# Cross-attention operands laid out and loaded per group of four sequences, three stage buffers, the loop written out

## The chip, the cores and the metric

The kernel runs on one core of one Trainium2 chip. The time is the device time in microseconds (us) of one execution; a profiled execution gives the span from the first to the last instruction. TensorE (PE) multiplies into PSUM, VectorE (DVE), ScalarE (ACT) and GpSimd (POOL) compute elementwise, and SyncE (SP) issues nearly all DMAs from one queue.

## The reference

One decoder layer over x of 32 sequences with 128 tokens and 128 features: linear attention, cross-attention on a context of 77 keys, and a mixture of 16 experts beside a shared expert. The part that the change touches is the cross-attention:

```python
def _feature_map(x, fm_w, fm_b):
    z = jnp.einsum('nshd,ed->nshe', x, fm_w) + fm_b
    return jnp.concatenate([jnp.exp(z), jnp.exp(-z)], axis=-1)      # 8 -> 16 features per head
v, k, q = (_feature_map(x, fm_w, fm_b) for x in (v, k, q))          # k and v from ctx_1024, q from x
scores = jnp.einsum('nqhd,nkhd->nhqk', q, k) / jnp.sqrt(jnp.float32(EMBED))
attn = jax.nn.softmax(scores, axis=-1)
out = jnp.einsum('nhql,nlhd->nqhd', attn, v).reshape(N, S, HEADS * EXP_DIM)
return out @ fc_w.T + fc_b
```

There are 16 heads with 16 features each after the map (`EX` in the kernel).

## The kernel before

Four phases run one after the other on every engine. Phase 1 (linear attention) goes over 8 groups of 4 sequences. Phase 2 computes the features of q and k, also in 8 groups of 4 (`JP`). Phase 3 is the cross-attention over 16 pairs of 2 sequences (`JA`, `NA`). Phase 4 is the mixture of experts.

Phase 2 writes each feature as a sum of `PARTS` = 3 bf16 numbers (high, middle, low), so that bf16 matmuls keep the precision. ACT computes the high parts, DVE the other parts of q, POOL those of k. The features come out with head and feature on the partitions (128 = 8 heads x 16, in two halves `hf`), but phase 3 wants the feature and the part on the partitions and the heads beside each other. The change of layout goes through DRAM: `sp_phase2` stores every group to `kparts` (L468, one DMA per part and half) and `qparts` (L473, one DMA per half), and `load_parts` reads them back for each pair. ACT may refill a part buffer only once its stores have landed (`q_sent`, `k_sent`; SP waits for all of them in `all_sent`, L485).

`load_parts` (L620) fills one of `NBUF` = 4 pairs of buffers `qst[r]`, `kst[r]`: 96 rows, which are 6 blocks of 16 features in the orders `Q_PART` = (0, 0, 0, 1, 1, 2) and `K_PART` = (0, 1, 2, 0, 1, 0), so that one matmul sums the six products of parts. It issues 6 DMAs for q (L624, each into 16 partitions, runs of 512 B) and 3 for k (L627, into 48, 32 and 16 partitions, runs of 308 B). Rows 96 to 98 (up to `SHIFT_ROWS`) carry the shift of the softmax: ones in `kst`, set once by POOL (L582), and in `qst` the negative row maxima, again in three parts.

All buffers of phase 3 lie in an arena `late`. Another arena, `early`, holds the scratch tiles of phase 1 and then those of phase 2 (`ctxT`, `kf`, `qpart`, `kpart`, residues).

Phase 3, in the order of PE: `step_a` of pairs 0 and 1 computes their scores (L661), of which DVE takes the maxima (L773) and makes parts of them; `turn_shift` (L670) transposes these, ACT copies them to `mT` (L833), and SP writes them by DMA into rows 96 to 98 of `qst` (L635, `shift`). `body(g)` first waits for `m_in` of its buffer, then computes the shifted scores (L691), from which ACT takes exp (L848), and the products with the values (L706); between them it computes the scores of pair g + 2 (`ahead`, which waits for `parts_in`) and turns the shift of pair g + 1. SP's `body(g)` waits until pair g - 1 is done (`bp`, L623), loads pair g + 3, and then writes the shift of g + 1, all in one queue. Ahead of that, in phase 2, `prefetch(0)` and `prefetch(1)` load pairs 0 and 1 before the stores of the last two groups. `loop3` (L606) writes bodies 0, 13, 14 and 15 out and has the others in a hardware loop of four.

POOL's `pool_phase3` copies the values of a sequence into `vcur` (L865), and adds the bias `fcb` to `xs` once (L869).

## Time and profile before

| | us |
|---|---|
| median of three runs | 703.36 |
| lowest and highest | 699.74, 706.22 |
| span of the profiled execution | 651.5 |
| PE busy, weight loads busy | 465.1, 320.6 |
| DVE, ACT, POOL busy | 341.3, 258.7, 202.1 |

Busy times lie beside each other, since the engines run at the same time. TensorE is busy for 71% of the span, but it is not the bound in every phase: which engine is late has to be read stage by stage, from what each one waits for. The DMA share is the mean busy share of the 16 DMA engines; it can be over 1 where packets overlap on one engine.

### The profile page before, as it was taken

What the parts mean: (1) busy time and instruction counts of PE and PEld (TensorE: products, weight loads), DVE (VectorE), ACT (ScalarE), POOL (GpSimd) and SP (SyncE); (2) the same over time, 40 slices, a digit from 0 to 9 for tenths busy, and PEclk for the clock granted to TensorE, in tenths of its full rate; (3) what the DMA queues carried; (4) which work ended last, traced back from release to release, by engine and by line L of the source; (5) the groups of instructions that cost most, each with busy time, mean ns of one, the idle gap of its engine ahead of it and who ended that gap; (6) DMA issues with size and microseconds to landing.
All of it is one profiled execution on the core that took longest, in us unless ns stands there. A gap on an engine that the chain in (4) does not pass through costs nothing.

```text
span 651.5 us, 12002 instructions
## 1 busy us (share of the span) xinstructions
PE 465.1 (71%) x3697; PEld 320.6 (49%) x3698; DVE 341.3 (52%) x969; ACT 258.7 (40%) x578; POOL 202.1 (31%) x271
## 2 busy tenths in 40 slices
PE   0576767665766128898898888895899999877720
PEld 0354544453433116566575666652356666665710
DVE  4547666532566924656556666647583333333322
ACT  0434444436886003434334444453653222333310
POOL 3123222163788500000000000002105760388850
PEclk9969686866888555959769989997989999889875
DMA  5820000000666997986679889000004110567727
GB/s 104 293 77 2 0 0 0 2 0 15 180 182 177 183 182 102 116 96 83 87 93 121 94 109 119 12 4 1 1 2 130 54 46 0 152 209 237 248 74 218
DMA packets 101544, 61.88 MB, mean 95 GB/s; under 512 B 33896, under 2 KB 99720, under 8 KB 101384
## 3 DMA queue, kind: packets, MB, share of 16 engines
q1 hardware_dynamic: 92040, 52.92, 42.6%
q0 software_dynamic: 2560, 5.31, 2.2%
q10 hardware_dynamic: 6912, 3.25, 2.1%
q8 instruction: 16, 0.26, 0.2%
q14 instruction: 16, 0.13, 0.1%
HBM read 40.34 MB, written 20.73 MB: 94 GB/s over the span
## 4 chain that ended last, share of the span: by engine, by line
PE 41%; DVE 17%; SPq 14%; ACT 9%; issue 8%; DMA 7%; POOL 2%; ACTq 1%; DVEq 0%; POOLq 0%
PE bank L706 5%; SPq L468 4%; PE bank L691 4%; PE bank L1177 4%; PE bank L1187 4%; PE bank L1188 4%; ACT prob L848 3%; SPq L1232 2%; PE bank L735 2%; PE bank L729 2%; DMA y_back<-routed 2%; PE bank L661 2%; PE bank L431 2%; PE bank L723 2%; PE bank L396 2%
## 5 line engine op out<-in xcount | busy, mean ns | idle before, releaser
L848 ACT ACTIVATE prob<-bank 77x512 f32<-77x512 f32 x128 | 73.7, 591 | 105.8 <-PE bank L691 105.4
L865 POOL COPY vcur<-vals 77x272 f32 (+1 forms) x32 | 13.1, 416 | 190.7 <-PE bank L706 190.7
L706 PE MATMUL bank<-prob,vcur 77*17 77x128 f32 x1024 | 58.7, 305 | 12.1 <-ACT prob L848 11.6
L661 PE MATMUL bank<-kst,qst 96*128 96x77 bf16 x512 | 41.8, 228 | 33.5 <-DMA kst<-kparts 24.1
L773 DVE TENSOR_REDUCE mx<-bank 128x5 f32<-128x385 f32 (+1 forms) x96 | 53.9, 580 | 22.1 <-PE bank L661 19.9
L691 PE MATMUL bank<-qst,kst 99*77 99x128 bf16 x512 | 58.7, 247 | 2.1 <-DMA qst<-mT 2.1
L820 DVE COPY avs_s<-bank 128x512 f32<-128x512 f32 x32 | 22.1, 691 | 57.9 <-PE bank L706 57.9
L691 PEld LDWEIGHTS bank<-qst,kst 99*77 99x77 bf16 x512 | 45.6, 135 | 11.3 <-issue 4.5
L661 PEld LDWEIGHTS bank<-kst,qst 96*128 96x128 bf16 x512 | 32.6, 117 | 37.0 <-DMA kst<-kparts 12.4
L1151 POOL DMA_INDIRECT routed<-t_y,t_no x48 | 47.2, 984 | 8.1 <-POOL carrier_p L1150 5.1
L936 DVE TENSOR_TENSOR act<-bank,s_g 128x512 f32<-128x512 f32 x32 | 22.0, 689 | 45.6 <-ACT s_g L1092 45.5
L380 POOL TENSOR_TENSOR qkv<-qkv,rn 128x256 f32<-128x256 f32 x32 | 19.1, 628 | 83.8 <-DVE rn L298 83.8
L1143 POOL DMA_INDIRECT sorted_in<-h_rows,pos_s x32 | 30.8, 964 | 41.7 <-issue 41.7
L1177 PEld LDWEIGHTS bank<-sd,act 128*128 128x128 f32 x256 | 33.7, 193 | 19.2 <-issue 13.4
L1092 ACT ACTIVATE s_g<-bank 128x512 f32<-128x512 f32 x32 | 19.0, 597 | 54.3 <-PE bank L1188 54.3
L409 PE MATMUL bank<-wqkv,xnT 128*128 128x384 f32 x64 | 32.8, 674 | 5.7 <-ACT xnT L339 5.7
L1177 PE MATMUL bank<-sd,act 128*128 128x128 f32 x256 | 34.6, 279 | 3.1 <-DVE act L936 3.1
L706 PEld LDWEIGHTS bank<-prob,vcur 77*17 77x17 f32 x1024 | 17.6, 98 | 35.2 <-ACT prob L848 23.2
L1027 DVE TENSOR_TENSOR t_act<-bank,t_sg 128x128 f32<-128x128 f32 x48 | 14.0, 291 | 39.0 <-ACT t_sg L1109 38.9
L1187 PE MATMUL bank<-xT,sg 128*128 (+1 forms) x64 | 33.7, 609 | 0.0
L1188 PE MATMUL bank<-xT,su 128*128 (+1 forms) x64 | 32.7, 592 | 0.0
L332 ACT ACTIVATE xn<-xs,ln_bias,ln_rstd 128x128 f32<-128x128 f32 (+1 forms) x64 | 26.4, 482 | 10.0 <-DVE ln_bias L280 9.7
(167 smaller groups left out, 1000.2 us busy)
## 6 DMA issues: line engine op xcount, KB each, us to landing
qst<-qparts SPq DMA_DIRECT2D x96, 128.0 KB, 4.5
t_w<-in_expert_w SPq DMA_DIRECT2D x48, 192.0 KB
qparts<-qpart SPq DMA_DIRECT2D x16, 384.0 KB, 3.4
kparts<-kpart SPq DMA_DIRECT2D x48, 77.0 KB
kst<-kparts SPq DMA_DIRECT2D x16, 231.0 KB, 6.6
sorted_in<-fill SPq DMA_DIRECT2D x1, 3168.0 KB, 10.5
t_row<-sorted_in ACTq DMA_DIRECT2D x48, 66.0 KB
kst<-kparts SPq DMA_DIRECT2D x16, 154.0 KB, 6.9
```

The source lines that it names most:

```text
L332: i = a.activation(dst[:, j], x_of(g, j), ACT.Identity, scale=ln_rstd[k][:, j:j + 1], bias=ln_bias[k][:, j:j + 1])
L409: pe.matmul(bank[1 + j][:, 0:3 * D], xnT[par][:, j * P:(j + 1) * P], wqkv[:], start=True, stop=True).then_inc(s["qkvp"], 1)
L661: i = pe.matmul(bank[n % 2][:, (h - h0) * KEYS:(h - h0 + 1) * KEYS], qst[r][0:ROWS, h, j * S:(j + 1) * S], kst[r][0:ROWS, h, j * KEYS:(j + ...
L691: i = pe.matmul(bank[2 + u % 2][0:KEYS, c * S:(c + 1) * S], kst[r][0:SHIFT_ROWS, h, j * KEYS:(j + 1) * KEYS], qst[r][0:SHIFT_ROWS, h, j * ...
L706: i = pe.matmul(bank[4][32 * c:32 * c + EX + 1, (u - 1) * P:u * P], av_lhs(g, r, j, 4 * (u - 1) + c), prob[(u - 1) % 2][:, c], start=True, ...
L773: v.tensor_reduce(mx[:, n // 3, h0:h1], bank[n % 2][:, 0:(h1 - h0) * KEYS].rearrange("p (h k) -> p h k", k=KEYS), AX.X, ALU.max).then_inc( ...
L848: a.activation(prob[u % 2][:].rearrange("p c t -> p (c t)"), bank[2 + u % 2][0:KEYS], ACT.Exp, scale=SCORE_SCALE).then_inc(s["expd"], 1)
L1143: p.indirect_dma_start(out=sorted_in, out_offset=bass.IndirectOffsetOnAxis(ap=pos[:, b:b + 1].bitcast(U32), axis=0), in_=h_rows[:, b], in_ ...
L1151: p.indirect_dma_start(out=routed, out_offset=bass.IndirectOffsetOnAxis(ap=t_no[r][:].bitcast(U32), axis=0), in_=t_y[r][:], in_offset=None ...
L1177: i = pe.matmul(bank[BK_DOWN[par]][:, j * D:(j + 1) * D], act[c][:, j * P:(j + 1) * P], sd[:, c], start=(c == 0 and j == 0), stop=(c == CH ...
L1187: pe.matmul(bank[BK_GATE[c % 2]][:], sg[:, c * P:(c + 1) * P], xT[:, bass.ds(g * GT, GT)], start=True, stop=True)
L1188: pe.matmul(bank[BK_UP[c % 2]][:], su[:, c * P:(c + 1) * P], xT[:, bass.ds(g * GT, GT)], start=True, stop=True).then_inc(s["gup"], 1)
```

## The change

`qparts` and `kparts` get the group of four sequences as their outermost dimension, and the heads and tokens of one feature and part lie side by side: 16 heads x 512 tokens x 2 B = 16 KB for q, 16 x 308 x 2 B = 9.9 KB for k. `load_parts` loads a whole group with 12 DMAs, each of 16 such runs into 16 partitions. The stores of q are now one DMA per part and half, as those of k. The buffers hold a group each, and there are three: two in `late`, the third in `early`, over the scratch of phase 2. For that reason the ones in its rows are set by POOL after the last store of phase 2, and its first load is issued behind `all_sent` and `vp`. `body(g)` loads group g // 2 + 2 when g is even, from 2 to 10. `loop3` is written out, all 16 bodies. `home`, `loads` and `shifts` give the buffer and the semaphore counts for a pair.

```diff
-    NBUF = 4
+    NBUF = 3
-        qparts = nc.dram_tensor("qparts", (HEADS, EX, PARTS, TOK), BF16).ap()
-        kparts = nc.dram_tensor("kparts", (PARTS, EX, HEADS, B * KEYS), BF16).ap()
+        qparts = nc.dram_tensor("qparts", (NG, EX, PARTS, HEADS, GT), BF16).ap()
+        kparts = nc.dram_tensor("kparts", (NG, EX, PARTS, HEADS, JK), BF16).ap()
...
-                        sp.dma_start(kparts[a, :, heads, bass.ds(g * JK, JK)].rearrange("e h t -> h e t"),
+                        sp.dma_start(kparts[bass.ds(g, 1), :, a, heads].rearrange("o e h t -> (o h) e t"),
                                      kpart[par][hf][:, a]).then_inc(k_sent[par][hf], 16)
...
-                    sp.dma_start(qparts[heads, :, :, bass.ds(g * GT, GT)].rearrange("h e a t -> (h e) a t"),
-                                 qpart[par][hf][:]).then_inc(q_sent[par][hf], 16)
+                    for a in range(PARTS):
+                        sp.dma_start(qparts[bass.ds(g, 1), :, a, heads].rearrange("o e h t -> (o h) e t"),
+                                     qpart[par][hf][:, a]).then_inc(q_sent[par][hf], 16)
...
-            for k in range(NBUF):
+            for k in range(NBUF - 1):
                 p.wait_ge(s["ones_rows"], k + 1)
                 p.memset(kst[k][ROWS:SHIFT_ROWS], 1.0).then_inc(s["ones_rows"], 1)
+            p.wait_ge(s["ones_rows"], NBUF)
+            loop2(p, body)
+            all_sent(p, NG // 2)
+            p.wait_ge(s["vp"], NG)
+            p.memset(kst[NBUF - 1][ROWS:SHIFT_ROWS], 1.0).then_inc(s["ones_rows"], 1)
             p.wait_ge(s["ones_rows"], 1 + NBUF)
-            loop2(p, body)
...
-        qst = [sb3(f"qst{i}", [SHIFT_ROWS, HEADS, JA * S], BF16) for i in range(NBUF)]
-        kst = [sb3(f"kst{i}", [SHIFT_ROWS, HEADS, JA * KEYS], BF16) for i in range(NBUF)]
+        stage = [sb3, sb3, early()]
+        qst = [place(f"qst{i}", [SHIFT_ROWS, HEADS, GT], BF16) for i, place in enumerate(stage)]
+        kst = [place(f"kst{i}", [SHIFT_ROWS, HEADS, JK], BF16) for i, place in enumerate(stage)]
...
-            step_a(0, 0, 0)
-            step_a(1, 1, 0)
-            body(0, 0, 0)
-            with eng.Fori(0, NA // NBUF - 1) as g4:
-                for r in range(NBUF):
-                    body(g4 * NBUF + (r + 1), (r + 1) % NBUF, g4 + (r + 1) // NBUF)
-            for g in range(NA - NBUF + 1, NA):
-                body(g, g % NBUF, g // NBUF)
+            step_a(0)
+            step_a(1)
+            for g in range(NA):
+                body(g)
+
+        def home(g, j):
+
+            return g // 2 % NBUF, (g % 2) * JA + j
...
             for at, part, n in Q_RUNS:
                 for i in range(n):
-                    sp.dma_start(qst[r][(at + i) * EX:(at + i + 1) * EX],
-                                 qparts[:, :, part, bass.ds(g * JA * S, JA * S)].rearrange("h e t -> e h t")).then_inc(parts_in[r], 16)
+                    sp.dma_start(qst[r][(at + i) * EX:(at + i + 1) * EX], qparts[group, :, part]).then_inc(parts_in[r], 16)
             for at, part, n in K_RUNS:
-                sp.dma_start(kst[r][at * EX:(at + n) * EX],
-                             kparts[part:part + n, :, :, bass.ds(g * JA * KEYS, JA * KEYS)].rearrange("a e h t -> (a e) h t")).then_inc(parts_in[r], 16)
+                for i in range(n):
+                    sp.dma_start(kst[r][(at + i) * EX:(at + i + 1) * EX], kparts[group, :, part + i]).then_inc(parts_in[r], 16)
...
                 if g == 0:
-                    shift(g, r)
-                    load_parts(sp, 2, 2)
+                    shift(g)
                     all_sent(sp, NG // 2)
-
-            def body(g, r, gb):
-                if not is_last(g, 3):
-                    if not (is_first(g)):
-                        sp.wait_ge(s["bp"], g * (4 * JA))
-                    load_parts(sp, g + 3, (r + 3) % NBUF)
-                if not is_last(g, 1):
-                    shift(g + 1, (r + 1) % NBUF)
+                    sp.wait_ge(s["vp"], NG)
+                    load_parts(sp, 2)
+
+            def body(g):
+                if g % 2 == 0 and 2 <= g < NA - 4:
+                    sp.wait_ge(s["bp"], g * (4 * JA))
+                    load_parts(sp, g // 2 + 2)
+                if g < NA - 1:
+                    shift(g + 1)
...
-            def body(g, r, gb):
-                pe.wait_ge(m_in[r], gb * (16 * JA) + 16 * JA)
+            def body(g):
+                pe.wait_ge(m_in[home(g, 0)[0]], shifts(g))
...
-            sp_phase2(sp, lambda g: load_parts(sp, g, g))
+            sp_phase2(sp, lambda g: load_parts(sp, g))
```

In every other place the change only renames `r` and the column of a sequence.

## Rows read from the trace of the kernel before

**Rows 1.** Timeline of SP: start us, us, engine, line, operation, count.

```profile
175.62 0.30 SPq L459 DMA_DIRECT2D ctx<-in_ctx  x1
176.20 4.82 SPq L468 DMA_DIRECT2D kparts<-kpart  x6
181.24 1.48 SPq L473 DMA_DIRECT2D qparts<-qpart  x2
...
190.69 0.30 SPq L459 DMA_DIRECT2D ctx<-in_ctx  x1
...
207.92 2.79 SPq L624 DMA_DIRECT2D qst<-qparts  x6
...
212.89 4.08 SPq L468 DMA_DIRECT2D kparts<-kpart  x6
...
256.92 2.81 SPq L624 DMA_DIRECT2D qst<-qparts  x6
...
263.87 1.60 SPq L635 DMA_DIRECT2D qst<-mT  x2
```

**Rows 2.** Waits of SP: us in total, times, longest us.

```profile
SPq L468 <- POOL kpart L576: 6.8, 1, 6.8
```

**Rows 3.** Waits of PE, same columns.

```profile
PE bank L661 <- DMA kst<-kparts: 24.1, 3, 12.2
```

**Rows 4.** Timeline of PE; then line L670: ns, first and last start.

```profile
219.13 0.88 PE L661 MATMUL bank<-kst,qst 96*128 96x77 bf16 x11 [12.16 <-DMA kst<-kparts]
...
237.50 0.65 PE L691 MATMUL bank<-qst,kst 99*77 99x128 bf16 x4 [2.06 <-DMA qst<-mT]
245.52 0.57 PE L661 MATMUL bank<-kst,qst 96*128 96x77 bf16 x6 [7.37 <-DMA kst<-kparts]
...
249.24 0.31 PE L670 MATMUL bank<-ident_b,mpart 128*128 128x128 bf16 x1
...
258.98 0.63 PE L691 MATMUL bank<-qst,kst 99*77 99x128 bf16 x4
...
L670 PE MATMUL bank<-ident_b,mpart x16: 221/221/314, 226.9 to 426.2; 128*128 128x128 bf16 x16
```

**Rows 5.** The line L624: ns min, median, max.

```profile
L624 SPq DMA_DIRECT2D qst<-qparts x96: 316/389/2117, 207.9 to 400.6; - x96
```

**Rows 6.** Windows: stretch, us, five engines busy (x), PEclk, DMA share, GB/s.

```profile
19.00:20.00 1.00, 0.00 (x0) 0.00 (x0) 0.00 (x0) 1.00 (x1) 0.00 (x0) 1.00 0.78 230
26.00:30.00 4.00, 4.00 (x11) 2.13 (x9) 1.83 (x4) 0.64 (x2) 1.26 (x1) 1.00 0.94 406
...
203.00:204.00 1.00, 0.91 (x4) 0.71 (x5) 1.00 (x3) 0.02 (x1) 0.23 (x1) 1.00 0.44 112
205.00:207.00 2.00, 1.98 (x11) 1.14 (x9) 0.05 (x1) 1.73 (x4) 1.66 (x3) 1.00 0.99 343
209.00:235.00 26.00, 5.73 (x62) 4.01 (x63) 19.93 (x21) 0.73 (x2) 12.16 (x7) 0.53 1.08 184
...
258.00:267.30 9.30, 8.80 (x119) 6.98 (x116) 6.67 (x21) 3.87 (x8) 0.82 (x2) 0.80 1.17 139
...
265.00:266.00 1.00, 1.00 (x20) 1.00 (x20) 0.92 (x3) 0.29 (x1) 0.41 (x1) 1.00 1.30 118
```

**Rows 7.** Lines L582 and L869 on POOL; timeline of DVE beside them.

```profile
L582 POOL MEMSET kst<- x4: 2146/2146/2147, 138.4 to 145.0; 3x2464 bf16 x4
...
L869 POOL TENSOR_TENSOR xs<-xs,fcb x1: 8797/8797/8797, 212.4 to 212.4; 128x4096 f32<-128x4096 f32 x1
...
210.98 11.33 DVE L560 TENSOR_TENSOR qpart<-res_q,qpart 128x512 bf16<-128x512 f32 x2
```

**Rows 8.** Windows of the cross-attention, columns as in rows 6.

```profile
275.00:295.00 20.00, 19.09 (x185) 13.89 (x181) 10.10 (x28) 6.89 (x16) 1.23 (x3) 0.51 0.80 92
...
340.00:355.00 15.00, 12.64 (x201) 9.00 (x201) 11.38 (x36) 6.87 (x14) 1.23 (x3) 1.00 1.02 126
...
415.00:430.00 15.00, 12.87 (x200) 8.77 (x200) 9.16 (x30) 7.29 (x16) 0.82 (x2) 1.00 0.02 4
```

More of the change, by code:

```diff
@@ L634, in shift, with step_a, scores @@
                     at = j * (PARTS + 1) * HEADS
-                    sp.dma_start(qst[r][ROWS:SHIFT_ROWS, :, j * S:(j + 1) * S], mT[r % 2][at:at + PARTS * HEADS]).then_inc(m_in[r], 16)
-            def step_a(g, r, gb):
+                    r, c = home(g, j)
+                    sp.dma_start(qst[r][ROWS:SHIFT_ROWS, :, c * S:(c + 1) * S], mT[g % 2][at:at + PARTS * HEADS]).then_inc(m_in[r], 16)
+            def step_a(g):
                 if g == 0:
-                    shift(g, r)
-                    load_parts(sp, 2, 2)
+                    shift(g)
                     all_sent(sp, NG // 2)
-            def body(g, r, gb):
-                if not is_last(g, 3):
-                    if not (is_first(g)):
-                        sp.wait_ge(s["bp"], g * (4 * JA))
-                    load_parts(sp, g + 3, (r + 3) % NBUF)
-                if not is_last(g, 1):
-                    shift(g + 1, (r + 1) % NBUF)
+                    sp.wait_ge(s["vp"], NG)
[6 more added lines that the diff above has]
+                    shift(g + 1)
             loop3(sp, body, step_a)
         def pe_phase3(pe):
-            def scores(g, r, j, u):
+            def scores(g, j, u):
+                r, c = home(g, j)
                 h0, h1 = UNITS[u]
@@ L661, in scores @@
                     i = pe.matmul(bank[n % 2][:, (h - h0) * KEYS:(h - h0 + 1) * KEYS],
-                                  qst[r][0:ROWS, h, j * S:(j + 1) * S], kst[r][0:ROWS, h, j * KEYS:(j + 1) * KEYS],
+                                  qst[r][0:ROWS, h, c * S:(c + 1) * S], kst[r][0:ROWS, h, c * KEYS:(c + 1) * KEYS],
                                   start=True, stop=True)
@@ L671, in turn_shift, with step_a, attend @@
                              ident_b[:]).then_inc(s["mTp"], 1)
-            def step_a(g, r, gb):
-                pe.wait_ge(parts_in[r], gb * LOADS + LOADS)
+            def step_a(g):
+                pe.wait_ge(parts_in[home(g, 0)[0]], loads(g))
                 for j in range(JA):
                     for u in range(len(UNITS)):
-                        scores(g, r, j, u)
+                        scores(g, j, u)
                 if g == 0:
                     turn_shift(g)
-            def attend(g, r, j, tails, ahead):
+            def attend(g, j, tails, ahead):
+                r, t = home(g, j)
                 for u in range(5):
@@ L691, in attend @@
                             i = pe.matmul(bank[2 + u % 2][0:KEYS, c * S:(c + 1) * S],
-                                          kst[r][0:SHIFT_ROWS, h, j * KEYS:(j + 1) * KEYS],
-                                          qst[r][0:SHIFT_ROWS, h, j * S:(j + 1) * S], start=True, stop=True)
+                                          kst[r][0:SHIFT_ROWS, h, t * KEYS:(t + 1) * KEYS],
+                                          qst[r][0:SHIFT_ROWS, h, t * S:(t + 1) * S], start=True, stop=True)
                         i.then_inc(s["bp"], 1)
@@ L713, in attend, with av_lhs @@
                         tails[2]()
-            def av_lhs(g, r, j, h):
-                return vcur[(r % 2) * JA + j][:, h]
+            def av_lhs(g, j, h):
+                return vcur[(g % 2) * JA + j][:, h]
             def tail(g, j):
@@ L747, in f @@
                         if j == 0 and u == 0 and more:
-                            pe.wait_ge(parts_in[rn_], gn * LOADS + LOADS)
+                            pe.wait_ge(parts_in[home(g + 2, 0)[0]], loads(g + 2))
                         if j == 0 and u == 3 and not is_last(g, 1):
@@ L751, in f @@
                         if more and u < len(UNITS):
-                            scores(g + 2, rn_, j, u)
+                            scores(g + 2, j, u)
                     return f
-                attend(g, r, 0, [] if first else tail(g - 1, 1), ahead(0))
-                attend(g, r, 1, tail(g, 0), ahead(1))
+                attend(g, 0, [] if first else tail(g - 1, 1), ahead(0))
+                attend(g, 1, tail(g, 0), ahead(1))
             pe.wait_ge(s["ones_rows"], 1 + NBUF)
@@ L805, in tail, with body @@
                     v.bn_stats(stats3[:, bass.ds(b, 1)].rearrange("p o f -> p (o f)"), x_b).then_inc(s["stat3"], 1)
-            def body(g, r, gb):
+            def body(g):
                 first = is_first(g)
@@ L830, in act_phase3, with copy_shift, step_a, body @@
         def act_phase3(a):
-            def copy_shift(g, r):
+            def copy_shift(g):
                 a.wait_ge(s["mTp"], g + 1)
-                a.copy(mT[r % 2][:], bank[5][:, 256:256 + S // 2].bitcast(BF16)).then_inc(s["mT"], 1)
-            def step_a(g, r, gb):
+                a.copy(mT[g % 2][:], bank[5][:, 256:256 + S // 2].bitcast(BF16)).then_inc(s["mT"], 1)
+            def step_a(g):
                 if g == 0:
-                    copy_shift(g, r)
-            def body(g, r, gb):
+                    copy_shift(g)
+            def body(g):
                 first = is_first(g)
```

22 lines of the change are left out of this document (13 added, 9 removed).

## Prediction

> **What bounds the kernel now.** I read the page first, then the waits of TensorE and of SyncE, then SyncE's timeline, and only then the bandwidth of single stretches. The profiled execution spans 651.5 us; the median of the runs is 703.4, so 51.9 us lie around the span, and I carry them over unchanged. The change touches two stages: the feature stage (about 153 to 235 us) and the cross-attention (219 to 443 us).
>
> In the feature stage nothing computes at its limit. SyncE's queue sets the pace. A group starts with its context load at 175.62 and the next but one at 190.69 [rows 1], so one group takes 7.5 us; of these the six stores of k take 4.82, the two of q 1.48, and the rest are the context load, register work and the loop. SyncE waited for klo only once in the whole stage [rows 2]: it is always late, and the engines wait for it through the "sent" semaphores.
>
> The cross-attention has one stall by DMA: three waits of scores, 24.1 us in total [rows 3]. The reader is to see where they lie: before the first scores at 219.13, and before 245.52, after the first attention unit at 237.50 [rows 4]; none lies after 245.52. So the loads are hidden in all the rest. From there the stage flows: the turn of the shift (L670) runs 16 times, from 226.9 to 426.2 [rows 4]. The second stands in body 0, at 249.24 [rows 4], so 14 bodies take 177 us, 12.6 us each.
>
> **Stores of q, in three DMAs each.** Per group SyncE issues six stores for q instead of two. They have the same three levels (head, feature, run) as the stores of k, so I price them as those: 4.82 us instead of 1.48, that is +3.34 us in each of the six groups ahead of the first prefetch, +20.0 us. Nothing covers this, because SyncE is what the stage waits for. The first prefetch then starts at 207.92 + 20.0 = 227.9 instead of 207.92 [rows 1]. The bounds: a simple load is issued in 389 ns [rows 5]; with about 130 ns of register work six would take 3.1 us, +1.6 per group, +9.9 in the six. Above k's price I see no reason to go.
>
> There is a second floor under this. In a stretch with k's stores alone the DMA engines are busy to 0.44 and move 112 GB/s; with q's stores as they are, 0.99 and 343 GB/s [rows 6]. A store with k's access pattern so runs on half of the engines. q's 0.79 MB per group at half of 343 take 4.6 us, k's 0.47 MB at 112 take 4.2: 8.8 us. So even with free issues the stage would lose 1.3 us per group; under the 10.9 that I forecast it doesn't count.
>
> **The prefetch at the end of the feature stage.** It now brings two groups of four sequences instead of two pairs. By the shapes a pair is six q loads of 131 KB and 473 KB of k, 1.26 MB; a group is 2.52 MB. From 209 to 235 the queue moved 4.8 MB at 184 GB/s with the engines busy over 1.0 [rows 6], which are the two pairs and the last two groups' stores. After, 2.52 MB more go through it, and the question on which most hangs is at which rate.
>
> In steady state the loads of a pair drain in 9.3 us at 139 GB/s, with a busy share of 1.17; 512-byte packets into all 128 partitions (the x loads at the start) give 230 GB/s at 0.78, and the store of `fill`, by its shape in rows of 25 KB, 406 at 0.94 [rows 6]. So the packet's size alone doesn't explain the 139. What both the old loads and the new ones have and the x loads haven't is the destination: 16 partitions per DMA (k's first two have 48 and 32; the new ones all have 16). So of the ends 139 and 406 I take the lower, the nearest row: a group drains in 18.6 us. The Trainium skill ("SBUF — State Buffer", "Door 1: The DMA port swizzle") says partitions 0 to 15 reach four of sixteen ports and measured 104 GB/s there; by it a group would take 24 us, and the sum below, with a group seven times on the path, would end 39 us later. No row here shows that number; the 139 is nearer to it than to 406.
>
> With 18.6 us the queue is empty at 235 + 20.0 + 18.6 = 273.6. SyncE's own issuing would end sooner: twice (12 loads in 6 by the 389 ns and 0.1 between them, k 4.08, q 4.08 by the price outside the loop [rows 1]) behind 227.9 is 256, and 259 with the last landing. So the queue decides in the forecast.
>
> **The start of cross-attention.** Before, PE needed only pair 0 and began at 219.13 [rows 4], ahead of the last stores. Now the third buffer lies in the feature stage's memory; its rows of ones are written by GpSimd only after all_sent, and PE waits for them (the last wait on ones_rows). The old memset of 2,464 elements took 2,146 ns [rows 7]; this one has 4,928, so 4.3 us. PE starts at 273.6 + 4.3 = 278. GpSimd then copies vcur (1.7 us) and adds fcb, 8.8 us [rows 7]. Beside that addition two DVE operations with two SBUF inputs took 11.33 us from start to end [rows 7]. Before, this met q's last residue, and was hidden by SyncE's lateness. Now it meets `parts(0)`: turn_shift(0) not before 278 + 10.5, then the copy, two issues and a landing, 4.5 us: body 0 at 293. Before, body 0 flowed from about 245 (one unit earlier, then the stall). That is +48 us; the 24.1 us of DMA waits are inside this difference and so are not a gain beside it.
>
> **The loads in the stage.** Per two bodies the same bytes, but in one piece: 12 loads at the start of body g = 2, 4, 6, 8, 10, and then, in the same queue, the shift rows for body g+1, without which PE may not begin it. Before, the loads were issued at 256.92 and the shift at 263.87 [rows 1], and the queue had drained by 268, well inside a body. Now: first issue to first packet 1.1, load 18.6, shift behind it 1.0: 20.7 us after the first issue. The old load was first issued at 256.92 and its body began at 258.98 [rows 1, 4], 2.1 us later. So an even body can't be shorter than 18.6 us against 12.6: +6.0, five times 30 us. The same holds for body 0, which has load 2 issued after shift 0: another 6. Sum 36 us. If loads run over 190 GB/s, this is nothing.
>
> **Edits at nothing.** The written-out loop: a looped stretch (340 to 355) had 201 matmuls and the already written-out one at 415 to 430 200, both at full clock [rows 8]; no branch time to win, no code loading to pay. Larger packets cost nothing. Four memsets of 2.1 become two of 4.3 ahead of the stage.
>
> **Sum:** +48 + 36 = +84 on the span: 735.5, and 735.5 + 51.9 = 787; I say 785.
>
> **The rivals.**
> Forecast, 0.58: as above. Its own range: at 118 GB/s, the slowest microsecond of a load [rows 6], a group takes 21.3 us, +2.7 seven times, 19 us; and where PE waits the granted clock may fall for the odd bodies. At 0.51 it issued 185 matmuls in 20 us, at 1.00 200 in 15 [rows 8]: with some 145 records in a body 15.7 us against 10.9; 5 odd bodies of 3 us more are 15. Downwards, overlap of loads on one half of the engines with stores on the other: 20 us. 765 to 820.
>
> Fast loads, 0.27: the new runs of 16 and 9.9 KB go at 250 to 406 GB/s, because short strided rows were the limit. For it: the k loads have short rows too and are as slow though spread over more partitions. Then only SyncE's issuing counts: 259 + 4.3 = 263.5, body 0 at 278.5, +34: 737. No waits in the stage. The Trainium skill ("DMA: Bandwidth & Descriptors", "Specifications") has 512 bytes as the least for full rate, which k's 308 bytes miss; it speaks for this rival. A rate near 190 gives about 746.
>
> Cheap issues, 0.08: the one-part stores of q cost 3.1 us per group and loads are fast: prefetch at 217.8, twice 13.2 us, landing 3.4, memset 4.3: PE at 252, body 0 at 267: +22, 725.
>
> Not slower, 0.07: the clock. In the stage it was 0.51 in 275 to 295 and 1.00 in 340 to 355 [rows 8]. If all 16 bodies ran at 10.9 instead of 12.6, 27 us come back. This decides only if the start slips by less than 27 us, which the cheap-issue case alone allows: 698 to 705. Against it: what the change does to the clock is to put waits in, not take any out behind 245.52. That the change does nothing is no rival: the wait on ones_rows alone moves PE's start behind the last store.
>
> **Range and chances.** 728 to 815 leaves out the cheapest case and the worst overlap of slow rate and clock. Measurement tells about 1% (7 us) from no change. Faster by over 1%: 0.03; within 1%: 0.04; slower: 0.93.
>
> **What would show it.** SyncE's period per group in the feature stage: 10.9 us (the three-level price), 8.8 (engines) or 7.5 (wrong). The windows in a prefetch: 130 GB/s or over 250. PE's first scores: 278, 264 or 252, released by GpSimd's memset and not by kst. The wait of L691 for qst<-mT in odd bodies: 6 us each, or none with fast loads. The forecast is wrong above all if these last waits are missing; its sign is wrong only if PE starts by 240.

## The result, and the profile after

The changed kernel takes 807.8 us (median of four runs, 807.2 to 810.0) beside 704.8 for the kernel before: ratio 1.146, 95% interval 1.140 to 1.152, or +103 us. The forecast was 785 with a range of 728 to 815. In a later comparison the unedited changed kernel took 765.2 beside 660.0 (ratio 1.160, 1.151 to 1.169): another level for both, and again +105. What the two levels are is told at the end of this section.

SyncE's queue in the changed kernel, as in [rows 1]: start us, us, line, operation, count.

```profile
194.53 0.31 SPq L459 DMA_DIRECT2D ctx<-in_ctx  x1
195.10 4.80 SPq L468 DMA_DIRECT2D kparts<-kpart  x6
200.10 4.74 SPq L474 DMA_DIRECT2D qparts<-qpart  x6
205.49 0.31 SPq L459 DMA_DIRECT2D ctx<-in_ctx  x1
...
229.17 2.66 SPq L638 DMA_DIRECT2D qst<-qparts  x6
...
238.75 13.66 SPq L474 DMA_DIRECT2D qparts<-qpart  x6
...
258.23 10.27 SPq L468 DMA_DIRECT2D kparts<-kpart  x6
268.54 9.85 SPq L474 DMA_DIRECT2D qparts<-qpart  x6
```

The reader sees a group take 10.96 us (194.53 to 205.49; 10.85 each over four groups), six stores of q at 4.74 instead of two at 1.48, and the first prefetch at 229.17. Behind it the same stores take 13.66, 10.27 and 9.85 us; I read this as SyncE standing in front of a full queue. From the first context load of the stage to the prefetch it is 74.3 us here and 54.7 in the profile of before. This distance repeats within 0.2 us in the other traces with the same stores (only run 11 is longer), so it is a better measure than the start alone, which moves by some us with the phase ahead of it.

GpSimd and TensorE at the start of cross-attention, timelines as in [rows 4]; the bracket is the idle time before, and who ended it:

```profile
284.01 4.20 POOL L588 MEMSET kst<- 3x4928 bf16 x1 [55.29 <-DMA qparts<-qpart]
...
289.71 8.81 POOL L883 TENSOR_TENSOR xs<-xs,fcb 128x4096 f32<-128x4096 f32 x1
...
288.27 0.90 PE L676 MATMUL bank<-kst,qst 96*128 96x77 bf16 x11 [61.01 <-POOL kst L588]
...
299.50 0.29 PE L685 MATMUL bank<-ident_b,mpart 128*128 128x128 bf16 x1 [7.58 <-DVE mpart L801]
...
303.19 0.65 PE L706 MATMUL bank<-qst,kst 99*77 99x128 bf16 x4
...
323.82 0.65 PE L706 MATMUL bank<-qst,kst 99*77 99x128 bf16 x4 [6.51 <-DMA qst<-mT]
```

TensorE waits 61 us for the memset of the ones, and the memset for the last store of q. Windows of the same trace, columns as in [rows 6]: the end of the feature stage in two parts, and from the second part a stretch with nothing but stores; then a load inside the cross-attention, once while TensorE works and once while it waits.

```profile
229.00:249.00 20.00, 0.00 (x0) 0.00 (x0) 2.57 (x5) 1.64 (x3) 0.00 (x0) 0.59 0.96 126
249.00:284.00 35.00, 0.00 (x0) 0.00 (x0) 0.00 (x0) 0.00 (x0) 0.00 (x0) 0.50 0.80 144
276.00:282.00 6.00, 0.00 (x0) 0.00 (x0) 0.00 (x0) 0.00 (x0) 0.00 (x0) 0.50 0.56 167
...
306.00:314.00 8.00, 7.71 (x86) 4.87 (x84) 3.69 (x7) 3.12 (x6) 0.41 (x1) 0.50 0.99 123
314.00:322.00 8.00, 3.19 (x26) 1.83 (x25) 2.17 (x9) 0.85 (x2) 0.41 (x1) 0.50 0.89 123
```

Waits of the changed kernel: us in total, times, the longest. The line answering to [rows 3] is gone, and a new one has come.

```profile
PE bank L706 <- DMA qst<-mT: 47.4, 6, 9.4
ACT s_g L1106 <- remote: 37.5, 3, 16.1
```

The turn of the shift, one per body, and the first transposes of the mixture of experts (L1176; L1162 in the kernel before): ns min, median, max, then first and last start.

```profile
L685 PE MATMUL bank<-ident_b,mpart x16: 221/300/314, 299.5 to 537.0; 128*128 128x128 bf16 x16
L1176 PE MATMUL bank<-ident_s,xn x32: 272/327/477, 560.3 to 575.5; 128*128 128x128 f32 x32
```

**Where the 103 us are.** The second turn starts at 307.37, at 249.24 before [rows 4]; the last one at 537.0, at 426.2 before. So body 0 comes 58 us later, and the 14 bodies between these turns take 229.6 us instead of 177: +53. The experts begin 111 us later than in the profile of before, all of it from these two stages. It is 111 and not 103 because cross-attention was quicker in that profile of before than in run 1, against which the sum comes out as 104.

**Two levels of time.** The second wait above, of ScalarE, lies in the mixture of experts, which the change doesn't touch. It is there in the same size (37.5 to 37.9 us) in seven other traces of this case, among them that of an unedited kernel before, in one more with 22.0 us, and missing in five, among them the profile of before that stood ahead of the prediction. The times split alike: the kernel before has medians of 703 to 705 beside the traces that have the wait and 660 beside those that don't. The wait belongs to the surroundings of a run, then, and not to a kernel; below each time stands beside its own run of before. A profile shows one execution, which in runs 3 and 11 is the longest one (770.6 and 771.1 us).

### The profile page after: what moved, and what is told of

Same layout as the page of the kernel before. It is cut to its first block, busy times and chain, and to the rows that moved or that the text cites. A ratio compares the mean times of both kernels' runs of the same rounds, so it can differ in the third digit from the quotient of the medians.

```text
span 806.3 us, 11339 instructions
## 1 busy us (share of the span) xinstructions
PE 499.5 (62%) x3698; PEld 340.8 (42%) x3698; DVE 332.5 (41%) x969; ACT 260.7 (32%) x578; POOL 199.6 (25%) x270
## 4 chain that ended last, share of the span: by engine, by line
PE 33%; SPq 17%; DMA 16%; DVE 13%; issue 7%; ACT 6%; another core or an unknown queue 5%; POOL 1%; ACTq 1%; POOLq 0%; DVEq 0%
DMA qst<-mT 11%; SPq L474 6%; SPq L468 5%; PE bank L706 4%; PE bank L721 3%; PE bank L1191 3%; PE bank L1201 2%; PE bank L1202 2%; PE bank L676 2%; SPq L1246 2%; PE bank L738 2%; DMA y_back<-routed 2%; PE bank L431 2%; PE bank L744 2%
## 5 line engine op out<-in xcount | busy, mean ns | idle before, releaser
L706 PE MATMUL bank<-qst,kst 99*77 99x128 bf16 x512 | 62.6, 259 | 47.4 <-DMA qst<-mT 47.4
L676 PE MATMUL bank<-kst,qst 96*128 96x77 bf16 x512 | 44.1, 236 | 64.1 <-POOL kst L588 61.0
L706 PEld LDWEIGHTS bank<-qst,kst 99*77 99x77 bf16 x512 | 48.2, 143 | 59.2 <-DMA qst<-mT 48.8
L721 PE MATMUL bank<-prob,vcur 77*17 77x128 f32 x1024 | 62.1, 321 | 11.7 <-ACT prob L862 10.6
L676 PEld LDWEIGHTS bank<-kst,qst 96*128 96x128 bf16 x512 | 35.4, 124 | 66.6 <-POOL kst L588 61.2
L1191 PEld LDWEIGHTS bank<-sd,act 128*128 128x128 f32 x256 | 35.6, 205 | 46.7 <-DVE act L950 34.6
L1191 PE MATMUL bank<-sd,act 128*128 128x128 f32 x256 | 37.2, 292 | 28.1 <-DVE act L950 28.1
L1201 PE MATMUL bank<-xT,sg 128*128 (+1 forms) x64 | 35.5, 639 | 0.0
L555 DVE TENSOR_TENSOR res_q<-qkv,qpart 128x512 f32<-128x512 f32 x16 | 13.1, 819 | 52.7 <-ACT qpart L530 52.7
L1202 PE MATMUL bank<-xT,su 128*128 (+1 forms) x64 | 34.7, 626 | 0.0
```

Of the source, the lines that this page charges most:

```text
L676: i = pe.matmul(bank[n % 2][:, (h - h0) * KEYS:(h - h0 + 1) * KEYS], qst[r][0:ROWS, h, c * S:(c + 1) * S], kst[r][0:ROWS, h, c * KEYS:(c + ...
L706: i = pe.matmul(bank[2 + u % 2][0:KEYS, c * S:(c + 1) * S], kst[r][0:SHIFT_ROWS, h, t * KEYS:(t + 1) * KEYS], qst[r][0:SHIFT_ROWS, h, t * ...
L721: i = pe.matmul(bank[4][32 * c:32 * c + EX + 1, (u - 1) * P:u * P], av_lhs(g, j, 4 * (u - 1) + c), prob[(u - 1) % 2][:, c], start=True, st ...
L1191: i = pe.matmul(bank[BK_DOWN[par]][:, j * D:(j + 1) * D], act[c][:, j * P:(j + 1) * P], sd[:, c], start=(c == 0 and j == 0), stop=(c == CH ...
L1201: pe.matmul(bank[BK_GATE[c % 2]][:], sg[:, c * P:(c + 1) * P], xT[:, bass.ds(g * GT, GT)], start=True, stop=True)
L1202: pe.matmul(bank[BK_UP[c % 2]][:], su[:, c * P:(c + 1) * P], xT[:, bass.ds(g * GT, GT)], start=True, stop=True).then_inc(s["gup"], 1)
```

## The experiments

Twelve kernels ran; in the quoted expectations they bear the names that stand in brackets.

**1 (c0). The kernel before once more**, nothing edited.

> The kernel before once more, unchanged, as a control. Its timed runs took 700 to 709 us, but its profiled execution spans only 651.5; the changed kernel's timed runs (807 to 810) and its profile (806.3) agree, and that profile has 39 us between 610 and 650 us, in the shared expert of phase 4, in which ScalarE stood 7.2, 14.2 and 16.1 us before three activations. Theory: this stall belongs to either kernel and was absent by chance in the profile of before; then this run takes about 704 us, its profile spans about 702, and the same line L1092 has waits of 7 to 16 us in phase 4, some 40 to 50 us in all. Rival: the stall is a consequence of the change; then the profile here has no wait of over 3 us at L1092 and its span is again 652, with 52 us outside it.

Measured 707.8 us beside 703.4, span 707.1. ScalarE's wait, then the turns:

```profile
ACT s_g L1092 <- remote: 37.9, 3, 23.4
...
L670 PE MATMUL bank<-ident_b,mpart x16: 221/221/314, 226.3 to 432.5; 128*128 128x128 bf16 x16
```

In every execution of this case that has both, the time is 1.8 us over the span (808.17 and 806.3 in the changed kernel), so no 51.9 us lie around it. One of the timed runs of before in the comparison of 9 to 11 has just the span of the first profile (653.3 us, span 651.5): that profile was of the kind without the wait. Of the 55.6 us between this span and 651.5, 37.9 are the wait, and 7.1 lie ahead of the experts, which begin at 456.6 instead of 449.5: the turns of this trace run from 246.78 to 432.51, 13.3 us a body, where the first profile had 12.6. The other 10.6 lie in the experts beside the wait, and no run here says what they are. Against this profile, the more usual one, the change costs +60.6 at the start (307.37 less 246.78) and +43.9 in 14 bodies: 104.5 beside the timed 103.

**2 (e3). The changed kernel with its loads spread over the partitions**, every sixth instead of 16 side by side; the same bytes, runs and number of DMAs. The blocks of part and feature interleave; the sum over rows is the same.

```diff
-                    sp.dma_start(qst[r][(at + i) * EX:(at + i + 1) * EX], qparts[group, :, part]).then_inc(parts_in[r], 16)
+                    sp.dma_start(qst[r][at + i:ROWS:len(Q_PART)], qparts[group, :, part]).then_inc(parts_in[r], 16)
```

The same is done for `kst`.

> The changed kernel, in which each load of 16 rows goes to partitions a step of 6 apart (row = 6 * feature + block, for q and k alike) instead of to 16 neighbouring ones. Run length, bytes, number of DMAs and the product are the same. Theory A (the destination's 16 neighbouring partitions hold the loads to about 122 to 139 GB/s): the loads go at over 250 GB/s, a group lands in 6 to 10 us, the waits for qst<-mT (47.4 us) vanish, PE starts some 15 to 25 us earlier: 715 to 745 us. Theory B (rows in memory or their number hold them): no change, 808 us.

Measured 737.2 us (726.5 to 741.5) beside 703.4. GpSimd's memset, the window of a load in its cross-attention, the wait that was 47.4, and the loads' time from issue to landing, here and in the changed kernel (line, count, KB each, us):

```profile
265.26 4.20 POOL L588 MEMSET kst<- 3x4928 bf16 x1 [39.55 <-DMA qparts<-qpart]
```

```profile
284.00:292.00 8.00, 7.71 (x90) 5.42 (x91) 4.75 (x12) 3.28 (x7) 0.41 (x1) 0.50 0.94 225
```

```profile
L706 PE MATMUL bank<-qst,kst 99*77 99x128 bf16 x512 | 58.7, 247 | 1.5 <-DMA qst<-mT 1.4
```

```profile
qst<-qparts SPq DMA_DIRECT2D x48, 256.0 KB, 5.1
kst<-kparts SPq DMA_DIRECT2D x48, 154.0 KB, 6.1
```

```profile
qst<-qparts SPq DMA_DIRECT2D x48, 256.0 KB, 9.3
kst<-kparts SPq DMA_DIRECT2D x48, 154.0 KB, 15.3
```

The load now runs at 225 GB/s instead of 123 (I had expected over 250), with the DMA engines as busy; the waits of TensorE for the shift fall from 47.4 to 1.4 us, the bodies to 12.4 us each (turns from 288.62 to 462.0), and TensorE starts at 269.52 instead of 288.27, since the drain behind the prefetch takes 38.5 us (226.81 to 265.26) instead of 54.8. That is 70 of the 103 us from one subscript: what held the rate at 123 is which partitions a DMA writes. Bytes, runs and the number of DMAs are the same in both kernels.

**3 (e4). Group loads in halves**, six DMAs at the even body and six at the odd one, into the same neighbouring partitions.

```diff
-                if g % 2 == 0 and 2 <= g < NA - 4:
+                if 2 <= g < NA - 4:
                     sp.wait_ge(s["bp"], g * (4 * JA))
-                    load_parts(sp, g // 2 + 2)
+                    load_parts(sp, g // 2 + 2, g % 2)
...
```

In the part left out, `load_parts` issues only the blocks of the half that is asked for.

> The changed kernel with the loads of a group inside the stage in two halves, blocks 0 to 2 in the even body and 3 to 5 in the odd one, so that the shift rows stand behind 1.26 MB instead of 2.52. Theory A (the shift queued behind a whole group costs 6 to 8 us per even body): the waits for qst<-mT fall from 47.4 to under 12 us (that of body 1, behind load 2, stays), time 765 to 775 us. Theory B (the loads themselves come too late, for whatever reason): the waits go over to L676 for qst or kst and the time stays within 1% of 808.

Measured 757.8 us (753.8 to 770.6), better than the 765 to 775 expected. In the profiled execution (770.6) TensorE's wait for the shift is 8.0 us in all, twice, instead of 47.4; the 14 bodies take 187.7 us (second turn at 305.86, last at 493.59: 13.4 each). Each load still writes 16 neighbouring partitions, and the pace is that of run 1: the shift no longer stands behind 2.52 MB, but behind half of it. So the loss in the stage needs both, the low rate and a load in one piece ahead of the shift.

**4 (e2). The wait for the ones put where the third buffer is first used**, at body 4; GpSimd's memset goes behind the addition of `fcb`.

```diff
+                if g == 4:
+                    pe.wait_ge(s["ones_rows"], 1 + NBUF)
...
-            pe.wait_ge(s["ones_rows"], 1 + NBUF)
+            pe.wait_ge(s["ones_rows"], NBUF)
...
```

> The changed kernel, but PE waits for the third buffer's ones only ahead of body 4, and GpSimd sets them behind the first copies of the values and the addition of fcb. Theory A (PE's start is tied to the last store and the memset): the scores of pairs 0 and 1 start when group 0 has landed, at about 250 instead of 288; body 0 still has to wait for the shift of pair 0, which SyncE issues behind the last stores, so it starts at about 287 instead of 303: 16 us less, 792 us. Theory B (queue alone): body 0 stays within 3 us of 303 and the time at 808.

Measured 804.2 us (790.4 to 812.7). Timeline of TensorE, its waits, and the whole window of the turns, here and in the changed kernel:

```profile
247.64 0.88 PE L672 MATMUL bank<-kst,qst 96*128 96x77 bf16 x11 [23.50 <-DMA kst<-kparts]
279.37 0.65 PE L702 MATMUL bank<-qst,kst 99*77 99x128 bf16 x4 [22.65 <-DMA qst<-mT]
```

```profile
PE bank L702 <- DMA qst<-mT: 62.1, 7, 22.6
```

```profile
253.00:523.00 270.00, 198.04 (x2152) 140.59 (x2156) 116.87 (x330) 77.35 (x157) 15.74 (x29) 0.61 0.51 72
```

```profile
300.00:537.00 237.00, 174.36 (x2144) 123.08 (x2141) 114.51 (x330) 76.06 (x157) 11.48 (x28) 0.72 0.50 67
```

TensorE begins 41 us earlier, but the first shift is queued behind the stores and loads of the feature stage, and body 0 is only 24 us earlier. The experts then begin at 546.6 instead of 560.3; 10 of the 24 us went in the bodies, at a granted clock of 0.61 instead of 0.72 and with 198 us of matmuls instead of 174 for nearly the same count. The time gained 3.6 us, inside the spread of its runs, where the two traces differ by 7.7. This was a miss: I had expected 792.

**5 (e5). The remedies of 2, 3 and 4 together.**

> The changed kernel with three edits together: loads to partitions a step of 6 apart, in halves inside the stage, and PE's wait for the third buffer's ones moved to body 4. Theory A (what is left of the loss over before is q's issuing, 20 us, and PE's start behind the last store): scores start at about 238, body 0 when the last stores and the shift of pair 0 have landed, about 266 instead of 284, time 718 to 722 us, still over before. Rival (an earlier start is given back by a lower granted clock, as the run with the moved wait alone hints): 728 to 737.

Measured 707.4 us beside 705.2: ratio 1.006, 1.002 to 1.010. The change is undone in its effect, though all its layouts, buffers and the written-out loop are still there. Together the three give 100 us; apart they gave 70, 50 and 4 (each beside the changed kernel of the first comparison). It is also 11 us under the lower end of what I had expected. Body 0 began about where I had put it (262.48, expected 266), so the miss lies in the bodies: the 14 of them take 167.5 us, 12.0 each, where the traces of before had 12.6 and 13.3. Two waits are left, the loads of the first group and the first shift behind the stores:

```profile
PE bank L676 <- DMA kst<-kparts: 15.1, 1, 15.1
PE bank L706 <- DMA qst<-mT: 15.1, 2, 15.0
```

**6 (e1b). From the kernel before, only the stores of q like those of k** (head outermost in the DMA, six instead of two). The loads of q read the new layout, in the same pieces.

```diff
-        qparts = nc.dram_tensor("qparts", (HEADS, EX, PARTS, TOK), BF16).ap()
+        qparts = nc.dram_tensor("qparts", (PARTS, EX, HEADS, TOK), BF16).ap()
...
-                    sp.dma_start(qparts[heads, :, :, bass.ds(g * GT, GT)].rearrange("h e a t -> (h e) a t"),
-                                 qpart[par][hf][:]).then_inc(q_sent[par][hf], 16)
+                    for a in range(PARTS):
+                        sp.dma_start(qparts[a, :, heads, bass.ds(g * GT, GT)].rearrange("e h t -> h e t"),
+                                     qpart[par][hf][:, a]).then_inc(q_sent[par][hf], 16)
...
```

> The kernel before with one part of the change alone: q is laid out as k is (part, feature, head, token) and stored by one DMA per part and half, six per group instead of two, each with the head outermost. Loads, buffers and loop are those of before. Theory A (SyncE's issuing is on the path, some 0.8 us each): a group takes 10.9 us instead of 7.5, the first prefetch starts at 229 instead of 208, the time is 704 + 18 to 21: 722 to 725 us. Rival (the stage has slack behind the stores, since the queue is full in the prefetch anyway): under 712 us.

Measured 723.0 us beside 705.2, ratio 1.026 (1.020 to 1.032). SyncE, two groups:

```profile
180.35 0.30 SPq L459 DMA_DIRECT2D ctx<-in_ctx  x1
180.94 4.82 SPq L468 DMA_DIRECT2D kparts<-kpart  x6
185.99 4.84 SPq L474 DMA_DIRECT2D qparts<-qpart  x6
191.05 0.31 SPq L459 DMA_DIRECT2D ctx<-in_ctx  x1
...
225.50 4.02 SPq L625 DMA_DIRECT2D qst<-qparts  x6
```

The period is 10.7 us here, 10.85 over four groups. From the first context load to the prefetch it is 74.2 us instead of 54.7: +19.5, and 17.8 are in the time. In the feature stage an issue is paid nearly in full. The issue of six loads of q took 4.02 us here and 2.79 before, so the edit isn't quite the stores alone.

**7 (e7). The other way: k stored like q**, one DMA per half, and six loads of 16 rows.

```diff
-        kparts = nc.dram_tensor("kparts", (PARTS, EX, HEADS, B * KEYS), BF16).ap()
+        kparts = nc.dram_tensor("kparts", (HEADS, EX, PARTS, B * KEYS), BF16).ap()
...
-                    for a in range(PARTS):
-                        sp.dma_start(kparts[a, :, heads, bass.ds(g * JK, JK)].rearrange("e h t -> h e t"),
-                                     kpart[par][hf][:, a]).then_inc(k_sent[par][hf], 16)
+                    sp.dma_start(kparts[heads, :, :, bass.ds(g * JK, JK)].rearrange("h e a t -> (h e) a t"),
+                                 kpart[par][hf][:]).then_inc(k_sent[par][hf], 16)
...
```

> The opposite edit on the kernel before: k laid out and stored as q is (head, feature, part, token), one DMA per half instead of three, and loaded by six DMAs of 16 neighbouring rows. SyncE then has 4 stores per group instead of 8. Theory A (SyncE's issuing bounds the feature stage at 7.5 us a group): the period falls to what ACT and GpSimd need, about 6.3 us, the first prefetch starts 7 to 9 us earlier, time 694 to 698. Rival (the chain through ACT, GpSimd and the landings takes 7.5 us by itself): 704, no change.

Measured 696.1 us beside 705.2, ratio 0.987 (0.982 to 0.992): faster than both kernels. SyncE, a group and the prefetch:

```profile
175.07 0.44 SPq L459 DMA_DIRECT2D ctx<-in_ctx  x1
178.77 1.52 SPq L467 DMA_DIRECT2D kparts<-kpart  x2
180.52 1.27 SPq L472 DMA_DIRECT2D qparts<-qpart  x2
182.42 0.30 SPq L459 DMA_DIRECT2D ctx<-in_ctx  x1
...
199.26 2.79 SPq L623 DMA_DIRECT2D qst<-qparts  x6
```

The issues fall to 3.2 us per group, but between the context load and k's stores SyncE now waits for GpSimd's part of k: the period is about 7 us instead of 7.5, where I had expected 6.3. The prefetch is 8.7 us earlier than in the profile of before, but 3.1 of these are there already when the stage begins. The stage itself gives 5.6 (49.1 us instead of 54.7 from the first context load), and the rest of the 9.1 in the time isn't accounted for.

**8 (e8). The same with loads to every sixth partition.**

> As e7_k_as_q, and every load of 16 rows goes to partitions a step of 6 apart; the runs stay short (512 and 308 bytes). Theory A (16 neighbouring partitions hold these loads too): the q loads go at over 200 GB/s, the waits for kst<-kparts and qst<-mT between 207 and 246 us fall from some 22 to under 12 us, time 684 to 690. Rival (runs of 308 and 512 bytes hold them at 130 to 140 GB/s, whatever the partitions): as e7_k_as_q.

Measured 696.9 us beside the same 705.2, ratio 0.987 (0.981 to 0.993): no better than 7, and 7 to 13 us over what I had expected. The loads did get faster (line, count, KB, us to landing; the kernel before had 4.5 for q and 6.6 and 6.9 for k):

```profile
qst<-qparts SPq DMA_DIRECT2D x96, 128.0 KB, 2.7
kst<-kparts SPq DMA_DIRECT2D x96, 77.0 KB, 2.5
```

But TensorE's first scores, at 207.94, must be followed by DVE's maxima, and DVE is held by this while GpSimd adds `fcb`:

```profile
206.00 11.33 DVE L559 TENSOR_TENSOR qpart<-res_q,qpart 128x512 bf16<-128x512 f32 x2
217.25 3.56 DVE L773 TENSOR_REDUCE mx<-bank 128x6 f32<-128x462 f32 x6
```

**9 (e9) and 10 (e10). GpSimd's addition moved ahead of its loop over the feature groups**, in 8 and in 7, with this edit:

```diff
+            p.wait_ge(s["xn2"], NG)
+            p.tensor_tensor(xs[:], xs[:], fcb[:].rearrange("p (o f) -> p o f", o=1).broadcast_to([P, B, D]),
+                            ALU.add).then_inc(s["xb2"], 1)
             loop2(p, body)
...
```

> This is the kernel e8 with one thing moved: GpSimd's addition of the bias to xs (8.8 us) runs before its loop over the groups of the feature stage, behind the last x, where GpSimd waits for data anyway. Theory (the addition holds DVE's maxima back at the start of cross-attention: in e8 a DVE wait of 9.1 us and an operation of 11.3 us at 206 to 217): the first turn of the shift comes about 7 us earlier (215 instead of 222), body 0 near 219, and 3 to 6 us of it reach the end: 690 to 694. Rival (something else is late next, the loads of the next pairs or the clock): the start of body 0 moves but the second turn stays where it is, and the time stays at 696 to 697.

> The kernel e7 with the same move of GpSimd's addition. In e7 the loads into neighbouring partitions still come late (17.8 us of waits for kst). If these loads set the second unit's start, the move gives nothing here (695 to 697) where it gives 3 to 6 us in e9; if the addition is the bound in both, both gain the same.

Measured beside a kernel before at 660.3: 646.7 us, ratio 0.983 (0.973 to 0.992), for the version of 8, and 647.4, ratio 0.988 (0.973 to 1.003), for that of 7. In 9 the pair of operations that took 11.33 us is quick:

```profile
210.11 1.70 DVE L559 TENSOR_TENSOR qpart<-res_q,qpart 128x512 bf16<-128x512 f32 x2
```

The first turn starts at 217.25 instead of 221.97, but the second turn at 239.43 instead of 237.75, behind a wait of 7.3 us for pair 2's loads (7.7 in run 8): these are late next. The intervals of 7, 8, 9 and 10 overlap, so no order among them is shown; the best that is shown is some 1.3 to 1.8% under the kernel before, and for version 10 alone the interval doesn't exclude no gain.

**11 (e11). The addition moved in the changed kernel alone.**

> The changed kernel with the same move and nothing else. The prediction put 10.5 us from PE's start to the first turn down to the addition beside DVE. Theory: the turn comes about 5 us behind PE's first scores instead of 11.2, so body 0 starts 5 to 6 us earlier, and since the loads in the stage set the pace of the pairs of bodies, all of it reaches the end: 801 to 803. Rival (the two scores units and maxima take these 11 us by themselves): no change, 807.

Measured 764.3 us (759.1 to 771.1) beside 660.3 (ratio 1.176, 1.162 to 1.189). The start of cross-attention went as expected, but the feature stage did not. GpSimd and SyncE at its beginning, then the start:

```profile
146.07 8.85 POOL L586 TENSOR_TENSOR xs<-xs,fcb 128x4096 f32<-128x4096 f32 x1 [1.53 <-ACT xn L332]
159.84 5.00 SPq L468 DMA_DIRECT2D kparts<-kpart  x6
...
285.37 0.90 PE L679 MATMUL bank<-kst,qst 96*128 96x77 bf16 x11 [60.63 <-POOL kst L591]
...
290.78 0.29 PE L688 MATMUL bank<-ident_b,mpart 128*128 128x128 bf16 x1 [1.75 <-DVE mpart L804]
...
294.45 0.65 PE L709 MATMUL bank<-qst,kst 99*77 99x128 bf16 x4
```

The turn is 5.4 us behind the first scores instead of 11.2, a gain of 5.8. But GpSimd is still adding when the first features of k are ready, and the first stores of k are issued 11.1 us after the first context load (148.74) instead of 7.3 in run 12 (149.02 to 156.33). SyncE sets the pace of this stage, so these 3.8 us are paid: the prefetch starts 78.0 us after the context load instead of 74.2. In run 9, where the edit delays the first stores as much, the stage keeps its length (49.2 and 49.1), since SyncE isn't its bound there. So only 2 of the 5.8 us reach body 0 (second turn at 298.64; run 12: 300.51). Behind it the 14 bodies take 235.4 us (run 12: 233.9), and TensorE stays at half clock to the end of the stage (534 to 550: 0.50; in run 12, 534 to 558: 0.92), so that the experts begin at 566.7 instead of 557.7. This profile is of an execution of 771.1 us, 7 over the median, so that last loss needn't be the edit's. The time shows no gain, and the spread of the runs would hide one of 2 us.

**12 (c1). The changed kernel once more.**

> The changed kernel once more, nothing edited. In the last comparison the kernel before took 660 us instead of 705, and its trace-mates have no wait of ScalarE for a remote queue in the mixture of experts. Theory (that stall of some 38 us comes with the chip, not with the kernel; the change costs the same 103 us with it and without): beside a kernel before at 705 the changed one takes 807, beside one at 660 it takes 763 to 770, the difference 101 to 107 us either way. Rival (the stall depends on when the kernel reaches the experts, which the change moves): the difference is near 140 or near 65.

Measured 765.2 us (763.0 to 773.2) beside 660.0; span 763.5, without the wait of ScalarE. The difference is 105.1 us, so the stall adds to the kernel and does not interact with the change. That it comes with the chip fell: this run was on the same chip as runs 5 to 8, where the kernel before took 705. The turns run from 292.6 to 534.4, the 14 bodies take 233.9 us and the experts begin at 557.7. Run 11, with 764.3, can't be told from this.

## Why the prediction was right, and where its steps were not

The forecast mechanism was the right one of the four, and the sign and the range held. The time was 21 us over the sum of 787 (23 over the 785 given). Beside the profile of before the two stages cost 111 us instead of 84: 10 more at the start and 17 more in the bodies. What lay outside them came to about 45 us and not to 51.9, which hid 7 of the 27.

**The price of the stores: right.** 10.9 us a group and +20.0 us to the prefetch were predicted; 10.85 and +19.7 were measured, counted from the first context load. Run 6 gives +19.5 for this edit nearly alone.

**The drain behind the prefetch: too short by 9 us.** The step took the 184 GB/s of [rows 6] for the old 26 us and added only the larger loads: queue empty 45.7 us after the prefetch's start. It took 54.8 (229.17 to 284.01). The bytes that I had counted were right. Two things were missing, and I can split them only by an estimate. The loads of two groups, 5.04 MB, take 41 us at the measured 123 GB/s where 139 gives 36.3: nearly 5 us. What is left for the 2.52 MB of stores is then 13.8 us instead of 9.4, 4.4 more, because the stores of q among them had changed their form too. I had priced this form one paragraph earlier ("second floor") at half of 343 GB/s and had not carried it over to the last two groups. The window 276 to 282, stores alone behind a full queue, bears that price out: 167 GB/s at a busy share of 0.56. The 112 GB/s of [rows 6], with which that paragraph priced k, need not be a limit of the queue: SyncE issued 77 KB every 0.80 us there, which is nearly 100 GB/s already. How much of the drain hangs on the loads' rate is shown by run 2, which has the same stores: it is 16.4 us shorter there.

**The memset and the addition: right.** 4.3 us predicted and 4.20 measured; TensorE's start to body 0, 15 predicted and 14.9 measured. That the addition on GpSimd holds DVE is shown by runs 8, 9 and 11: without it the turn comes 5.4 us after the scores.

**The rate of the loads: right in kind, optimistic in size.** I took 139 GB/s, the rate of loads that partly wrote 48 and 32 partitions; with all twelve DMAs on 16 partitions it is 123. 2.52 MB then take 20.5 us, and the six bodies behind a load take 21.3 us each from turn to turn (the last of them 482.0 to 503.4), where I had 18.6; the other eight take 12.7, as before. Six times 2.7 us are 16, and that is nearly the whole step from the predicted +36 to the measured +53. (Run 12 has 233.9 us for the same bodies and run 1 has 185.7 for the old ones, so with other pairs of traces the 53 is anything from 44 to 57.) The fast-loads rival, 0.27, needed 250 GB/s. It fell with the changed kernel itself, and run 2 says why: longer runs did not help, another destination did. The Trainium skill ("SBUF — State Buffer", "Door 1: The DMA port swizzle") has 104 GB/s for partitions 0 to 15 and counts four ports of sixteen there; the order of this agrees, the runs give 123 and lie between it and my value. By its table the 16 partitions with a step of six reach 13 or 14 ports. The measured rate rises to 225, in the direction of the table but by much less than the number of ports.

**"51.9 us lie around the span": wrong.** 1.8 us do. The profiled execution of before was none of the three timed ones; it had no wait of ScalarE of 38 us and a quick cross-attention, and the median was of executions slower by 50. That the step did no harm was luck: the changed kernel's trace has the wait too, so that to carry the difference over happened to count it. Beside runs without the wait the changed kernel takes 765 us (run 12). The gap had no row behind it, and I gave it a name all the same.

**The written-out loop: at nothing, and nothing speaks against it.** No run undoes it alone. In run 5, which has it, a body takes 12.0 us, so it can't cost much.

**The stage's clock.** The forecast let a lower clock in waiting bodies only widen the range. It moves more than that: for the same changed kernel the granted clock over the bodies was 0.72 and 0.68 in two traces and the 14 bodies took 229.6 and 233.9 us. Run 4 began body 0 24 us earlier and lost 10 of them in bodies at 0.61. That an early start must be paid back so isn't shown, since no run varied the clock alone.

What stays open: what ScalarE's remote wait is. It lay in three pieces of different length with a sum of 37.5 to 37.9 us (22.0 in two pieces in run 8), beside GpSimd's indirect DMAs in the experts; in six traces (the changed kernel's and those of runs 1, 2, 5, 7 and 8) its last piece ended some 6 us after the last of these DMAs was issued. The profile of before has the same DMAs and no such wait, so they alone aren't the cause. No run here was made to find it.

## What to carry to other kernels

Before loads are made larger, look at the bandwidth of the old ones at a busy share near 1: if it is far below what other transfers reach there, the limit may be where they write, and then longer runs change nothing, as here. To spread each DMA over the partitions, by letting blocks interleave, is one subscript and cheap to try. A small transfer that gates the next step (here the shift, two DMAs of 12 KB) must not be queued behind a large prefetch, so a prefetch in two halves can be better than one with longer runs. And a DMA's form is a price at every place where it stands: if a store's layout changes, recompute all stretches that it runs through, the drain at the end first. A rate read from a stretch in which the issuing engine was the bound is no price of the queue. Last, work moved out of one stage can hold another up: look at the stage that receives it.

## What the runs showed of the hardware

- Twelve DMAs of 16 runs of 16 or 9.9 KB into 16 neighbouring partitions move 123 GB/s at a busy share of 0.99; into every sixth partition, 225 GB/s at 0.94. In these rows the busy share says nothing of the rate.
- Stores with 8 heads outermost, alone behind a full queue, moved 167 GB/s at a busy share of 0.56; those with head and feature merged 343 at 0.99 [rows 6].
- Short runs were not what held the loads here: with 308-byte and 512-byte runs, loads to every sixth partition landed in 2.5 and 2.7 us (run 8) where those to neighbouring ones took 6.3 and 4.5 (run 7). The Trainium skill ("DMA: Bandwidth & Descriptors", "Specifications") asks for 512 bytes for the full rate. That these loads would be faster still with longer runs isn't excluded.
- The issue on SyncE has a price by the form of the destination as well: six loads took 2.66 us into neighbouring partitions and 3.82 into every sixth (run 2).
- GpSimd's 8.8 us addition, with inputs in SBUF, stretches a pair of DVE operations from 1.70 us to 11.33. The Trainium skill ("SBUF — State Buffer", "SBUF: two separate sides") has it as an exclusive lock of a port pair; these numbers agree.
- The granted clock over the bodies was 0.72, 0.68 and 0.61 in the changed kernel, in run 12 and in run 4, which all have long waits between bodies, and 0.80 in run 2, which has none. The same 2,141 to 2,152 matmuls took 174, 183, 198 and 163 us there. The waits aren't all of it: run 1, without them, stands at 0.75.
